# One maximum over a pair of PSUM banks in two attentions, with four banks for the maxima's scores and two for the exponentials'

## The reference

```python
# L0: q, k and v are the same projection; heads are cut out of the token axis
qh = (x @ wq.T + bq).reshape(16, 4, 512, 8)
attn = softmax(einsum('hbqd,hbkd->hbqk', qh, qh) / sqrt(128))
x = x + einsum('hbqk,hbkd->hbqd', attn, qh).reshape(4, 512, 128) @ wu.T + bu

# L3: keys in four blocks of 128, each with a maximum m of its own (over its 128 keys)
for k_blk, v_blk in blocks:
    s = einsum('bhqd,bhkd->bhqk', q, k_blk) * 8 ** -0.5
    m = max(s, axis=-1); e = exp(s - m)
    num += e @ v_blk; den += sum(e)
x = x + (num / den) @ w_o
```

## Time and profile before

| | |
|---|---|
| median of 3 runs | 1765.02 us (1763.72 to 1772.39) |
| profiled execution, its own time | 1762.92 us |
| its span | 1761.0 us |
| mean granted TensorE clock | 0.93 |
| the two attentions in the span | about 190 to 425 us and 1385 to 1620 us |

### The profile page before, as it was taken

How to read it: one execution, slowest core, us unless ns; L and a number is a source line. 1 busy time by engine, 2 the same in 40 slices (tenths; PEclk the granted TensorE clock), 3 DMA queues, 4 the chain that set the end, 5 groups by cost and what they waited for, 6 DMA issues and landing times. The chain is left out here.

```text
span 1761.0 us, 25128 instructions
## 1 busy us (share of the span) xinstructions
PE 1517.7 (86%) x8766; PEld 1042.4 (59%) x8766; DVE 1230.0 (70%) x2815; ACT 1022.9 (58%) x1826; POOL 610.4 (35%) x738
## 2 busy tenths in 40 slices
PE   5999799998799799849999977997696799997696
PEld 4777323333577588637888965897696422222695
DVE  6687778994778744473535967596786778884785
ACT  3553478887554455345537732774374488887374
POOL 2675311121387200023006733673423211111423
PEclk9999989999899899969999988898798899999898
DMA  3121634400221400010000000000564633300564
GB/s 115 50 73 32 119 45 55 55 1 1 82 73 41 140 23 1 0 40 9 1 1 12 1 1 1 1 1 1 156 188 139 161 64 55 54 1 1 158 197 146
DMA packets 100757, 101.05 MB, mean 57 GB/s; under 512 B 23344, under 2 KB 86360, under 8 KB 99769
## 3 DMA queue, kind: packets, MB, share of 16 engines
q1 hardware_dynamic: 97687, 93.39, 21.7%
q0 software_dynamic: 2944, 6.05, 1.0%
HBM read 87.60 MB, written 15.78 MB: 59 GB/s over the span
## 5 line engine op out<-in xcount | busy, mean ns | idle before, releaser
L2636 DVE TENSOR_REDUCE mx<-bank 128x1 f32<-128x512 f32 (+1 forms) x512 | 320.2, 680 | 60.1 <-PE bank L2427 59.2
L2573 ACT ACTIVATE e<-bank 128x512 f32<-128x512 f32 x512 | 273.1, 599 | 53.6 <-PE bank L2459 50.7
L2459 PE MATMUL bank<-qq,kk 99*128 99x512 bf16 (+1 forms) x512 | 166.3, 391 | 13.4 <-ACT e L2573 12.8
L1565 POOL TENSOR_TENSOR midl<-mid,midh 128x512 fp32r<-128x512 f32 (+1 forms) x96 | 137.3, 1442 | 67.7 <-ACT midh L1485 67.4
L2459 PEld LDWEIGHTS bank<-qq,kk 99*128 99x128 bf16 (+1 forms) x512 | 39.3, 98 | 163.8 <-ACT e L2573 121.3
L1068 DVE TENSOR_TENSOR hl<-q,hh 128x512 fp32r<-128x512 f32 x64 | 44.8, 700 | 125.6 <-ACT hh L1038 103.7
L96 PE MATMUL bank<-wdh,midh 128*128 128x256 f32 (+1 forms) x384 | 113.8, 296 | 10.1 <-DVE x L1549 9.7
L227 POOL TENSOR_SCALAR rs<-mv 128x4 f32<-128x4 f32 x48 | 12.7, 265 | 288.4 <-DVE mv L214 287.5
L98 PE MATMUL bank<-wdh,midl 128*128 128x256 f32 (+1 forms) x384 | 110.9, 289 | 0.0
L97 PE MATMUL bank<-wdl,midh 128*128 128x256 f32 (+1 forms) x384 | 110.7, 288 | 0.0
L1480 ACT ACTIVATE mid<-bank,bu 128x512 f32<-128x512 f32 (+1 forms) x96 | 65.9, 687 | 64.8 <-PE bank L98 60.2
(11 more groups left out here) (406 smaller groups left out, 4429.2 us busy)
## 6 DMA issues: line engine op xcount, KB each, us to landing
w<-in_L_ffn_W SPq DMA_DIRECT2D x30, 512.0 KB
w<-in_L_ffn_W SPq DMA_DIRECT2D x30, 256.0 KB
qq<-scratch SPq DMA_DIRECT2D x18, 384.0 KB
w<-in_L_ffn_w_kernel SPq DMA_DIRECT2D x16, 344.0 KB
w<-in_L_ffn_w_kernel SPq DMA_DIRECT2D x16, 320.0 KB
wo<-in_L_ffn_wo_kernel SPq DMA_DIRECT2D x16, 320.0 KB
scratch<-e SPq DMA_DIRECT2D x34, 128.0 KB, 4.3
sorted<-in_unsorted SPq DMA_DIRECT2D x2, 1935.0 KB, 11.0
```

What stands on the lines that cost most here:

```text
L1565: e.tensor_tensor(l[0:fn, o], mid[i % 2][0:fn, o], h[0:fn, o].bitcast(F32), ALU.subtract).then_inc(*l2_m_lo.tick(n, i, f))
L2459: e.matmul(b_bank(t, u, j), keys(kk[0:K], t, b)[:, k * 128:(k + 1) * 128], queries(qq[0:K], t, b), start=True, stop=True).then_inc(*at_b.t ...
L2573: e.activation(er[u][:, j * 512:(j + 1) * 512], b_bank(t, u, j), ACT.Exp, bias=0.0, scale=scale).then_inc(*at_e.tick(n, t, u, j))
L2636: e.tensor_reduce(mxa[t % 3][:, o:o + nkb], bank[place_a["a", t, u, j]].rearrange("p (k n) -> p k n", k=nkb), X, ALU.max).then_inc(*at_max ...
```

## The change

One `tensor_reduce` over a pair of banks (1024 columns) replaces two over one bank each; A's pairs turn through `wide[0]` and `wide[1]`, banks 0 to 3, with one semaphore step a unit. B's products go to banks 4 and 5, the first of a unit always to 4 and the second to 5, and each waits for the exponential two back. On TensorE a unit's B and A products alternate: B0, A0, B1, A1. The output and its transpose take the first bank of one of A's two pairs. The projection of the values turns through two banks.

```diff
-                    uses_a += [("a", i, u, 0), ("a", i, u, 1)]
+                    uses_a += [("a", i, u)]
...
-            place_a, before_a = turns(uses_a, 3)
+            place_a, before_a = turns(uses_a, 2)
...
-            b_bank = lambda t, u, j: bank[3 + (16 * t + 2 * u + j) % 3]
-            b_before = lambda t, u, j: (16 * t + 2 * u + j - 3) // 2
+            b_bank = lambda t, u, j: bank[4 + j]
+            a_bank = lambda *use: wide[place_a[use]][:, 0:512]
...
-                    if c >= 3:
-                        q.wait_ge(*ve_set.at(n, c - 3))
+                    if c >= 2:
+                        q.wait_ge(*ve_set.at(n, c - 2))
...
-                        a = e.matmul(bank[3 + c % 3][:, j * 128:(j + 1) * 128], ...)
+                        a = e.matmul(bank[4 + c % 2][:, j * 128:(j + 1) * 128], ...)
...
-                def stage_a(t, u):
+                def stage_a(t, u, j):
...
-                    for j in range(2):
-                        p = bank[place_a["a", t, u, j]]
-                        f = before_a["a", t, u, j]
+                    if j == 0:
+                        pieces_ready(q, t)
+                        f = before_a["a", t, u]
...
+                    a = e.matmul(wide[place_a["a", t, u]][:, j * 512:(j + 1) * 512], l[:, qt * 128:(qt + 1) * 128], r, ...)
+                    if j == 1:
+                        a.then_inc(*at_a.tick(n, t, u))
...
-                def stage_b(t, u):
+                def stage_b(t, u, j):
...
-                    for j in range(2):
-                        f = b_before(t, u, j)
-                        if f >= 0:
-                            q.wait_ge(*at_e.at(n, f // 8, f % 8, (16 * t + 2 * u + j - 3) % 2))
+                    f = 8 * t + u - 1
+                    if f >= 0:
+                        q.wait_ge(*at_e.at(n, f // 8, f % 8, j))
...
                     if s == "a":
-                        stage_a(i, u)
-                        if 8 * i + u < AHEAD:
+                        k = 8 * i + u - AHEAD
+                        stage_a(i, u, 0)
+                        if k >= 0:
+                            stage_b(k // 8, k % 8, 1)
+                        stage_a(i, u, 1)
+                        if k < 0:
                             keep_warm(q, bank[6], 3)
...
                     elif s == "b":
-                        stage_b(i, u)
+                        stage_b(i, u, 0)
+                        if 8 * i + u + AHEAD >= 128:
+                            stage_b(i, u, 1)
...
-                    for j in range(2):
-                        o = (b * 4 + 2 * half + j) * nkb
-                        q.wait_ge(*at_a.at(n, t, u, j))
-                        e.tensor_reduce(mxa[t % 3][:, o:o + nkb], bank[place_a["a", t, u, j]].rearrange("p (k n) -> p k n", k=nkb), X,
-                                        ALU.max).then_inc(*at_max.tick(n, t, u, j))
+                    o = (b * 4 + 2 * half) * nkb
+                    q.wait_ge(*at_a.at(n, t, u))
+                    e.tensor_reduce(mxa[t % 3][:, o:o + 2 * nkb], wide[place_a["a", t, u]].rearrange("p (k n) -> p k n", k=2 * nkb), X,
+                                    ALU.max).then_inc(*at_max.tick(n, t, u))
```

More of the change, by code:

```diff
@@ L2407, in project_v @@
                 def project_v(c):
-                    if c >= 3:
-                        q.wait_ge(*ve_set.at(n, c - 3))
+                    if c >= 2:
+                        q.wait_ge(*ve_set.at(n, c - 2))
                     for j in range(4):
                         t = 4 * c + j
-                        a = e.matmul(bank[3 + c % 3][:, j * 128:(j + 1) * 128], xT[:, t * 128:(t + 1) * 128], wv, start=True, stop=True)
+                        a = e.matmul(bank[4 + c % 2][:, j * 128:(j + 1) * 128], xT[:, t * 128:(t + 1) * 128], wv, start=True, stop=True)
                     a.then_inc(*ve_mm.tick(n, c))
-                def stage_a(t, u):
+                def stage_a(t, u, j):
                     qq, kk = pieces[(t // 4) % 2]
                     b, half = u // 2, u % 2
-                    pieces_ready(q, t)
-                    for j in range(2):
-                        p = bank[place_a["a", t, u, j]]
-                        f = before_a["a", t, u, j]
+                    if j == 0:
+                        pieces_ready(q, t)
+                        f = before_a["a", t, u]
                         if f:
                             q.wait_ge(*(xsum.at(m, f[1]) if f[0] == "out" else (at_max if f[0] == "a" else at_oT).at(n, *f[1:])))
[L2424 to L2427, removed]
+                    qt = 2 * half + j
+                    l, r = (keys(kk[0:72], t, b), queries(qq[0:72], t, b)) if kind == 0 else (
+                        queries(qq[0:72], t, b), keys(kk[0:72], t, b))
+                    a = e.matmul(wide[place_a["a", t, u]][:, j * 512:(j + 1) * 512], l[:, qt * 128:(qt + 1) * 128], r, start=True, stop=True)
+                    if j == 1:
+                        a.then_inc(*at_a.tick(n, t, u))
                 def put(t):
@@ L2453, in stage_b @@
                     q.wait_ge(*at_mrow.at(n, t, b))
-                    for j in range(2):
-                        f = b_before(t, u, j)
-                        if f >= 0:
-                            q.wait_ge(*at_e.at(n, f // 8, f % 8, (16 * t + 2 * u + j - 3) % 2))
-                        k = 2 * half + j
-                        e.matmul(b_bank(t, u, j), keys(kk[0:K], t, b)[:, k * 128:(k + 1) * 128], queries(qq[0:K], t, b), start=True,
-                                 stop=True).then_inc(*at_b.tick(n, t, u, j))
+                    f = 8 * t + u - 1
+                    if f >= 0:
+                        q.wait_ge(*at_e.at(n, f // 8, f % 8, j))
+                    k = 2 * half + j
+                    e.matmul(b_bank(t, u, j), keys(kk[0:K], t, b)[:, k * 128:(k + 1) * 128], queries(qq[0:K], t, b), start=True,
+                             stop=True).then_inc(*at_b.tick(n, t, u, j))
                 def stage_o(t, k):
@@ L2516, in pe @@
                         q.wait_ge(*at_max.at(n, *f[1:]))
-                        turn(i, bank[place_a["turn", i]])
+                        turn(i, a_bank("turn", i))
                     elif s == "out":
@@ L2520, in pe @@
                         q.wait_ge(*at_max.at(n, *f[1:]))
-                        put_out(i, bank[place_a["out", i]], otr[i % 2])
+                        put_out(i, a_bank("out", i), otr[i % 2])
                     elif s == "finish":
                         finish_pe(q, m, i, stage, nxt)
-                q.wait_ge(*at_max.at(n, 15, 7, 1))
+                q.wait_ge(*at_max.at(n, 15, 7))
                 q.wait_ge(*at_e.at(n, 15, 7, 1))
@@ L2677, in dve @@
                     elif s == "out":
-                        add(i, bank[place_a["out", i]])
+                        add(i, a_bank("out", i))
                     elif s == "finish":
@@ L2716, in split @@
                     v = lambda z: z.rearrange("p (b k n) -> p b k n", b=4, k=4)
-                    q.wait_ge(*at_max.at(n, t, 7, 1))
+                    q.wait_ge(*at_max.at(n, t, 7))
                     if t >= 2:
```

2 lines of the change are left out of this document (1 added, 1 removed).

## The result

The changed kernel takes 1783.18 us (median of five runs, 1782.29 to 1787.43); the kernel before took 1768.27 beside it (1763.72 to 1772.39). The ratio is 1.0094, 95% interval 1.007 to 1.0118: slower, as forecast, but by 0.94% where the forecast was 0.6%. The profiled executions are 19.5 us apart in span (1761.0 and 1780.5).

What follows compares the result with a forecast made beforehand. No engine leads: a round is a chain of maximum, split, spreads, exponentials, one B, values product. First attention +4.7, second +6.4, together +11.1 on 1762.9 gives 1774.0; with 2.1 for the median, 1776 us; range 1757 to 1784.

Steps and rivals of the forecast that it cites:

- the ring step: Exponentials' banks 3 to 2: B1 waits for the second exponential of the unit before, not the first, 0.49 us later.
- The rival in which the maxima decide: B1's wait is off the path, so waits for maxima and head time come back: -14, 1751 us; chance 0.15.
- Interleaving: TensorE's order: one A instead of two lies between B1 and the product with the values, 0.22 us less.
- +0.16 for the split: Pair maximum can't begin before A1, so GpSimd's split starts at B0 + 2.40 us against + 2.24.
- The maximum's size: One maximum over 1024 columns on VectorE takes 1.21 us, within bounds of 1.07 and 1.36.
- -0.5 for the other two: Second and third chunk-finishing rounds of each attention: VectorE bounds them, its 0.56 us saving counts, so -0.5 us each.
- hidden: A's four banks as two pairs: A0's wait for the pair two units back is covered in a plain round.
- the first attention's rounds: Plain rounds pass the ring wait twice, +0.27 each less about 0.13: 12.60 becomes 13.02 us.
- a vanishing wait: First attention's plain rounds: faster VectorE removes about 0.13 us of waiting for a maximum ahead of the values product.
- The heads: 15 units of A alone, bound by VectorE: -0.6 us in the first attention, nothing in the second.
- The clock rival: One more stretch at 1.2 GHz in each attention, +5 and some +3 us: 1784 us; chance 0.08.
- Tails: 15 units without A: the fourth B waits for a later exponential, two units take 2.86 us, +2.4 us an attention.

Runs made afterwards that it cites:

- the first and fourth experiments: First: kernel before with only the exponentials' banks cut from three to two, 1.0149. Fourth: changed kernel with two single-bank maxima a unit, 1.0061.
- the fourth experiment: Changed kernel with two maxima of 512 columns a unit in place of one of 1024: 1777.27 us, 1.0061 to the kernel before.
- the spare products: Seven spare products of 416 columns ahead of the first place, here added to the kernel before with interleaved order: 1774.43 us beside 1779.94, 0.9967.

## Why the prediction was right in direction and short in size

**What belongs to the base.** 1783.18 lies 7.2 us above the 1776 forecast. Of these, 3.3 are the kernel before's own: it took 1768.27 beside the changed kernel and 1765.02 in the runs that the forecast stood on. The other 3.9 are the change's, +14.9 against +11.0.

**The chain and the ring step: right.** The round was read as a chain with one B in it, and its forecasts of 13.27 (second attention) and 2.86 (a tail's pair) measured 13.27 and 2.87. The rival in which the maxima decide falls: A's waits did vanish (13.5 us to 0.9) and the plain rounds still grew.

**The terms of that sum: right, with a link that only the experiments showed.** The ring was put at +0.49, which is what it measures at its own link (2.88 less 2.39). Interleaving was put at -0.22; it gives that ahead of O, and 0.21 again ahead of the split (2.23 with the ring alone, 2.02 with single maxima interleaved), which the prediction had inside its +0.16 for the split. Against single maxima in the same order the pair maximum brings the split 0.38 later, which makes up the 0.16. What the prediction did not have is the link from place to spread. It grows by up to 0.18 us where ScalarE is still in its exponentials when the place is done, as in the first and fourth experiments. In the changed kernel the split comes late enough for ScalarE to be free, the link is 0.42 as before, and so the sum came out.

**The maximum's size: right.** 1.21 us from the line through 128 and 512 columns; it measures 1.216. Its cost is also the forecast's mechanism, being late rather than long.

**The failed step: finishing rounds, "-0.5 for the other two".** The prediction took VectorE as the bound of every finishing round and let the pair maximum's 0.56 us count there. The second one fell, from 14.63 to 14.24 and from 14.42 to 14.14, and the third grew, from 14.67 to 15.41 and from 14.63 to 15.29: +0.7 instead of -0.5, 2.4 us in two attentions. Neither follows the mechanism that was forecast.

*The second finishing round: near the number by luck.* In the kernel before, an A product waited there for a maximum:

```profile
343.08 0.39 PE L2427 MATMUL bank<-qq,kk 72*128 72x512 bf16 x1 [1.19 <-DVE mx L2636]
```

The load ahead of it waited 1.7 us, A's longest wait from 230 to 400 us. With a fourth bank for A the longest such wait in this round is 0.6 us. It is the bank that shortens the round, and not the pair maximum: with two single maxima on the same four banks (the fourth experiment) it is shorter still, 14.01 us by these splits, and 13.65 in the second attention, against 14.24 and 14.14 changed.

```profile
345.17 0.31 POOL L2728 TENSOR_SCALAR mpt<-mx 128x16 bf16<-128x16 f32 x1 [6.43 <-DVE mx L2641]
...
359.18 0.33 POOL L2728 TENSOR_SCALAR mpt<-mx 128x16 bf16<-128x16 f32 x1 [6.12 <-DVE mx L2641]
```

So in this order the cheaper maximum gave back nothing even where VectorE was busiest, and A's fourth bank, which the prediction put at nothing ("hidden"), was worth more than 0.4 us: with ring, order and bank against order alone, 14.01 and 13.65 against 14.59 and 14.09. No run gave A the fourth bank and left B its three, since six banks don't allow it.

*The third finishing round: held by ScalarE.* The one in the first attention of the changed kernel, whose split starts at 398.44:

```profile
400.24 0.66 PE L193 MATMUL bank<-cf,xn 128*128 128x128 f32 x4
400.93 0.59 ACT L267 COPY xT<-bank 128x512 f32<-128x512 f32 x1 [1.20 <-PE bank L193]
...
401.42 0.62 ACT L425 CAST xn1r<-xn 128x512 fp32r<-128x512 f32 x1
...
401.61 0.39 PE L2435 MATMUL bank<-cb,mpt 128*128 128x128 bf16 x4
...
401.93 1.09 ACT L2579 ACTIVATE e<-bank 128x512 f32<-128x512 f32 x2
...
403.05 0.57 ACT L2562 CAST qq<-bank 3x512 bf16<-3x512 f32 x1
```

ScalarE has a copy and a cast for the next stage ahead of the round's exponentials, 1.00 us (400.93 to 401.93) that the second finishing round doesn't have. Link by link: from split to place it is 3.17 us here and 2.68 in the second round, from place to the first spread 1.44 against 0.65, together 1.28 more; from that spread to the next split 10.80 against 10.91. The rounds differ by 1.17. The place's load waits there for ScalarE's copy, and the spread stands behind the exponentials that the copy and the cast put off. So this round is longer ahead of the spreads, and not among the maxima. The kernel before has the same delay, 4.29 us from split to first spread against 3.02, and there both rounds lasted 14.6 us for different reasons: the second by A's wait for VectorE, the third by ScalarE, whose idle time ahead of the exponentials is 0.9 us in the third (and 1.1 ahead of the copy) against 3.1 in the second. A round held by ScalarE's chain gets nothing from a cheaper maximum and pays the ring and the late maximum in full. The variants agree: in the second attention this round takes 15.12 with the ring alone and 14.92 with ring, interleaving and single maxima, against 14.63 before and 15.29 changed. So the ring is +0.5 of it (15.12 less 14.63) and the pair maximum +0.37 (15.29 less 14.92), less 0.2 for the interleaving with A's fourth bank. That the copy and the cast are what sets this round apart is argued from these links; no run took them out.

**Mis-sized: the first attention's rounds.** Plain ones measure 13.11 against 13.02. The experiments divide the +0.51: +0.94 for the ring (13.54), -0.44 for the interleaving with A's fourth bank (13.10), +0.01 for the pair maximum. The forecast was +0.54 for ring and order, less 0.13 for a vanishing wait; that last term is the one that hardly came (0.03 of it, if the 0.54 holds). Rounds with an output transpose gained 0.52 against 0.4, the first finishing rounds of the two attentions 0.54 and 0.63 against 0.4. Together with the 0.3 us that the second finishing rounds lack to -0.5 each, these are 1.7 us; their links were not followed one by one.

**The heads: they differ by execution.** The forecast had -0.2 to the first attention's third split and +0.4 to the second's; +0.5 and +1.2 were measured. But from the first split to the third the same changed kernel took 30.52, 30.40 and 28.14 us in the first attention, at granted clocks of 0.72, 0.72 and 0.88, and 27.42, 24.52 and 29.65 in the second (0.81, 1.00 and 0.77); the kernel before took 29.75 (0.77) and 26.96 (0.87). The spread of 5 us in the second is larger than what was to be read. What repeats is the way from the first product to the first split: 10.53, 10.54 and 10.53 us in the first attention against 10.83 before (-0.3), and 14.61, 14.34 and 14.48 in the second against 13.85 in the one execution of before. The clock rival fits in part: the changed kernel had one more stretch of lower clock in the first attention's head each time, but removing it moved no total that could be measured.

**Tails.** +2.2 each against +2.4.

## What to carry to other kernels

Before banks are moved between two rings, find for each ring which work waits for the product that would wait: here B stands on the chain and A beside it, so the bank taken from B cost 0.65 us in a round of 12.85. The one given to A removed waits that held nothing in the plain rounds, and it shortened the one round in which VectorE had most to do. A reduce over two banks saves little of its length and starts only when the second bank is full; here it did not pay even in those rounds. The cheap part of this change, the order alone, was what gained in the total: interleave with the ring of three, and the kernel is 0.4% faster (0.9958, and 0.9967 on a second chip with the spare products in it).

Rounds that last equally long need not share a bound (14.63 and 14.67 us here): look at every engine's extra instructions and its idle time in each kind before one saving is multiplied by their number.

## What the runs showed of the hardware

- A maximum over 1024 columns in two adjoining banks took 1216 ns, over 512 columns 680 ns. Back to back they take less: nine single ones took 5.47 us in the head before (0.60 apart), six wide ones 6.88 us after (1.13 apart). So the width saves 0.07 us on a pair in a full queue.
- In the first attention's head TensorE waits for the first split. In the five profiled executions in which it waited 1.74 to 1.81 us, the granted clock from 204 to 218 us was 0.76 or 0.88; in the eight in which it waited 1.51 us or less, it was 1.00. In the changed kernel it was 1.00 from 236 to 420 and from 1440 to 1600 us. Over the whole kernel the loss in the head could not be told from none.
- The rounds of the changed kernel behind the third split repeat to 0.02 us from execution to execution and chip to chip, while medians of the kernel before lie from 1762.12 to 1779.94. One exception was met: two rounds of the interleaved kernel were 2.0 and some 4.2 us longer in one execution. Read parts from the rounds and totals from ratios.
